# Two eight-expert stages on sorted rows, with their routing streamed behind the attention ahead of each

## The chip, the cores and the metric

The kernel runs on one core of a Trainium2 chip. The metric is the device time of one launch in microseconds (us). Engines are called as in the profile: PE (TensorE, matrix products; PEld is its weight load), DVE (VectorE), ACT (ScalarE), POOL (GpSimd), SP (SyncE, which issues most DMAs).

## The reference

Four layers run over x, 2048 tokens (8 x 256) of 128 channels. Each layer adds an attention and then a mixture of experts, both on a layer norm of x:

```python
x = x + _L1_xattn_ref(_layernorm(x), ctx, ctx, mask_bk, ...)   # 16 heads of 64, 64 keys
x = x + _L1_ffn_ref(_layernorm(x), ...)                        # 8 experts, F = 512, 2 picked
x = x + _L2_xattn_ref(_layernorm(x), ctx, ...)                 # 16 heads of 8, 64 keys
x = x + _L2_ffn_ref(_layernorm(x), ...)                        # 8 experts, F = 256, 2 picked
```

Layers 0 (narrow attention, self attention and four mixed experts) and 3 (two-way attention, 64 experts of which 6 are picked) are computed as before by both kernels. An eight-expert mixture is, for each token, the sum over its two picked experts i of

```python
h = silu(x @ w1[i]) * (x @ w3[i])
out = out + (h @ w2[i]) * wi[..., None]
```

where the two weights wi come from a softmax over the two highest gate logits.

## The kernel before

The tokens are 16 tiles of 128 rows, kept in SBUF as `x`. The program is a sequence of blocks. In a block each engine has its own program, written by hand, in the order in which it runs; engines wait for each other by semaphores, and a block ends when all its engines are done. Expert products use fp32r: each operand is split into a high part (ACT, a copy) and a low part (DVE, the difference), and three matmuls give the product.

The blocks around the change:

- `attend_wide` (L844), the attention of layer 1, runs over the tiles in steps, with stages of up to four later steps for one tile (`rotate`, L250, a loop). In one step PE does query products of tile t (L904), eight transposes of tile t-3 (L912, into a `ps_t` of 1024 columns), scores of tile t-1 (L922, L926), and the output product of tile t-4 (L936). DVE takes maxima and sums and ends with the add to `x` (L1018). POOL divides the softmax (`t_sm` times `t_den`, L892).
- `normalise` n5 then makes the layer norm of all rows (DVE L134, L167), turns it (PE L228), makes gate logits (PE L217), and loads the first expert weights.
- `experts_sorted` e1 (L2069): DVE picks two experts per token for all 16 tiles together (L2300 to L2316), PE counts them (L2194), DVE works out places and the table of blocks (L2320 to L2357). POOL then writes every row twice into a DRAM buffer, `sorted`, by 32 indirect DMAs (L2175), one per tile and pick. The buffer holds 39 blocks of 128 rows, each for one expert, and was filled with blank rows in the first attention (L2954). ACT and DVE (L2065, L2066) split the weights of eight experts meanwhile. When all rows have landed, SP loads batches of three blocks (`e_zb`, L2147). For each batch PE turns the rows (L2203) and they are split (DVE L2364). For each block PE multiplies up (L2215 to L2217), ACT does silu, DVE multiplies (L2374), PE turns the result (L2225), ACT and DVE split it, PE multiplies down (L2236 to L2240), DVE adds (L2387), and POOL writes the 128 rows back to the order of tokens by an indirect DMA (L2182). At the end SP reads them back (L2154) and DVE adds them to `x` (L2394).
- `open_small` n6 and `attend_small` t2 (L566) are the attention of layer 2, over eight sequences b of two tiles, with stages of up to three later steps. The last operation of a tile is DVE's add (L796).
- `normalise` n7 and `experts_gated` e2 (L1745) follow: every expert runs over all tokens in four groups of 512, with the gate multiplied in; the weights stream in and are split on the way.
- `normalise` n8 follows, and in it ACT splits the first piece of layer 3's expert weights (L2555), whose load SP issued in e2.

## Time and profile before

| | us |
|---|---|
| median of 3 runs | 1537.43 (1535.21 to 1538.8) |
| the profiled execution | 1535.73 |
| its span, first to last instruction | 1533.9 |
| attend_wide | 523.6 to 651.4 |
| n5, then e1 | 651.7 to 668.8, 669 to 870.8 |
| n6, then t2 | 872 to 892.8, 894 to 966.5 |
| n7, then e2 | 966.8 to 987.5, 987.8 to 1136.3 |

Busy time over the span is PE 1252.8 us (82%), DVE 954.1 (62%), ACT 717.2 (47%) and POOL 627.5 (41%); the mean granted clock of TensorE is 0.893 of full speed. These shares are averages over stages of different limits, so a stage is read by its own window. In a row of the timeline the bracket gives the idle time of that engine ahead of the instruction and what ended it.

### The profile page before, as it was taken

To read this page: it belongs to the slowest core of one execution; us is meant where nothing else is said; L and a number is where in the kernel's file an instruction comes from. 1 tells how busy PE (TensorE), PEld (TensorE's weight loads), DVE (VectorE), ACT (ScalarE), POOL (GpSimd) and SP (SyncE) were. 2 spreads that over 40 slices of the span, in tenths; PEclk is the share of its full clock that TensorE was granted. 3 is DMA by queue.
4 is the path that set the end of the run, shared out by engine and by line. 5 is a ranking of instruction groups with operands and counts; after the bars stand their busy time and mean duration, and the time that the engine had idled before them with its cause. 6 is when DMAs were issued, how large, how long until landed. Compare 5 with 4: busy or idle time off the path is not lost. (4 is left out here: it accounts for less than half of the span.)

```text
span 1533.9 us, 24119 instructions
## 1 busy us (share of the span) xinstructions
PE 1252.8 (82%) x7202; PEld 1023.8 (67%) x7202; DVE 954.1 (62%) x1956; ACT 717.2 (47%) x1258; POOL 627.5 (41%) x638
## 2 busy tenths in 40 slices
PE   5986489997997899930899489699968559999997
PEld 3873379996654599920788358588846447787875
DVE  5546688887324376561565555667767567677775
ACT  2444456675332445431455245355543435555553
POOL 3204444430000133227233332269947236666665
PEclk9997789998898899955899789699988679999998
DMA  7900010110000000032111260032213034343433
GB/s 199 223 1 0 13 45 26 41 36 6 0 1 0 21 2 0 0 130 88 40 46 41 65 163 1 21 100 91 79 57 128 1 90 127 114 128 119 124 116 103
DMA packets 77809, 99.14 MB, mean 65 GB/s; under 512 B 15242, under 2 KB 41741, under 8 KB 77722
## 3 DMA queue, kind: packets, MB, share of 16 engines
q1 hardware_dynamic: 74018, 92.95, 21.3%
q0 software_dynamic: 2272, 4.24, 0.8%
q10 hardware_dynamic: 1440, 0.98, 0.3%
q8 instruction: 39, 0.64, 0.2%
q14 instruction: 40, 0.33, 0.1%
HBM read 78.14 MB, written 14.16 MB: 60 GB/s over the span
## 5 line engine op out<-in xcount | busy, mean ns | idle before, releaser
L2742 POOL TENSOR_TENSOR e_h<-e_h,e_gate 128x512 f32<-128x512 f32 x128 | 187.8, 1484 | 135.4 <-DVE e_h L2794 87.3
L2799 DVE TENSOR_TENSOR e_h_low<-e_h,e_h_high 128x512 fp32r<-128x512 f32 x132 | 117.2, 888 | 77.5 <-ACT e_h_high L2729 77.3
L2729 ACT ACTIVATE e_h_high<-e_h 128x512 fp32r<-128x512 f32 x132 | 83.5, 633 | 102.8 <-POOL e_h L2742 94.7
L1320 PE MATMUL u_ps_o<-u_vaug,u_pT 128*128 128x72 f32 x768 | 97.1, 270 | 0.0
L2794 DVE TENSOR_TENSOR e_h<-e_s,e_ps_b 128x512 f32<-128x512 f32 x132 | 89.3, 677 | 10.3 <-ACT e_s L2714 5.5
L1320 PEld LDWEIGHTS u_ps_o<-u_vaug,u_pT 128*128 128x128 f32 x768 | 93.6, 192 | 0.0
L2714 ACT ACTIVATE e_s<-e_ps_a 128x512 f32<-128x512 f32 x132 | 77.5, 587 | 25.7 <-PE e_ps_a L1742 23.3
L1251 POOL TENSOR_TENSOR u_kbd<-u_keys,groupmask 96x512 fp32r<-96x512 f32 x60 | 62.8, 1067 | 62.5 <-DMA u_keys<-s_k 37.0
L1347 ACT ACTIVATE u_sm<-u_sm 128x512 f32<-128x512 f32 x96 | 60.6, 631 | 53.4 <-DVE u_sm L1379 52.8
L1377 DVE TENSOR_REDUCE u_mx<-u_ps_s 128x2 f32<-128x512 f32 (+1 forms) x96 | 66.2, 689 | 21.2 <-PE u_ps_s L1302 20.3
L228 PE MATMUL n_ps_t<-ident,n_zn 128*128 128x128 f32 x96 | 25.9, 433 | 61.6 <-DVE n_zn L167 53.8
L2182 POOL DMA_INDIRECT sorted_y<-e_y,e_zb x39 | 37.8, 970 | 91.2 <-DVE e_y L2387 88.7
L879 POOL MEMSET t_vbd<- 128x1024 f32 x1 | 1.0, 951 | 171.0 <-POOLq L816 171.0
L1379 DVE TENSOR_TENSOR u_sm<-u_ps_s,u_mx 128x512 f32<-128x512 f32 x96 | 66.4, 692 | 7.1
L1958 ACT ACTIVATE e_s<-e_ps_a 128x512 f32<-128x512 f32 x64 | 38.3, 599 | 58.3 <-PE e_ps_a L1742 58.3
L892 POOL TENSOR_TENSOR t_sm<-t_sm,t_den 128x1024 f32<-128x1024 f32 x16 | 30.4, 1901 | 82.3 <-DVE t_den L1004 82.3
L228 PEld LDWEIGHTS n_ps_t<-ident,n_zn 128*128 128x128 f32 x96 | 18.2, 226 | 67.3 <-DVE n_zn L167 59.2
L666 PE MATMUL t_ps_o<-a_vaug,t_pT 128*128 128x72 f32 x512 | 61.5, 273 | 0.0
L1343 ACT ACTIVATE u_pT<-u_ps_t 128x512 f32<-128x512 f32 x96 | 57.2, 595 | 8.3 <-PE u_ps_t L1308 6.4
L323 POOL TENSOR_TENSOR a_kbd<-a_k,groupmask 96x1024 fp32r<-96x1024 f32 x16 | 30.2, 1890 | 74.5 <-PE t_ps_t L653 60.3
L666 PEld LDWEIGHTS t_ps_o<-a_vaug,t_pT 128*128 128x128 f32 x512 | 59.9, 192 | 0.3
L1740 PE MATMUL e_ps_y<-e_h_high,ed_low 128*128 128x512 f32 x132 | 52.9, 400 | 8.5 <-DVE e_y L2803 5.5
(501 smaller groups left out, 3868.9 us busy)
## 6 DMA issues: line engine op xcount, KB each, us to landing
e_gate<-gates_by_expert SPq DMA_DIRECT2D x256, 128.0 KB, 2.9
e_gate<-gates_by_expert SPq DMA_DIRECT2D x32, 256.0 KB, 3.2
a_q<-q_part SPq DMA_DIRECT2D x24, 256.0 KB, 6.5
w_raw<-in_L1w SPq DMA_DIRECT2D x24, 256.0 KB, 4.1
u_qs<-s_q SPq DMA_DIRECT2D x16, 192.0 KB, 2.6
u_keys<-s_k SPq DMA_DIRECT2D x8, 384.0 KB, 3.5
w_w<-in_L2w SPq DMA_DIRECT2D x24, 128.0 KB, 2.6
sorted<-blank SPq DMA_DIRECT2D x1, 2535.0 KB, 16.5
```

Of the source, the lines that this page charges most:

```text
L666: last = nc.tensor.matmul(ps_o[:, a * NA:(a + 1) * NA], pT[b % 2][:, j, t * P:(t + 1) * P], vaug[b % 2][:, a, pair * NA:(pair + 1) * NA], ...
L1251: return eng.tensor_tensor(kbd[:, HG * g:HG * (g + 1), kb * P:(kb + 1) * P], keys[:, kb, g, :].unsqueeze(1).broadcast_to([ROWS, HG, P]), g ...
L1320: last = nc.tensor.matmul(ps_o[par][:, a * NA:(a + 1) * NA], pT[(r - 3) % 2][:, i, :], vaug[kb][:, a, own * NA:(own + 1) * NA], start=own ...
L1343: nc.scalar.activation(pT[r % 2][:, :, :].rearrange("p a b -> p (a b)"), ps_t[r % 2][:, :], ACT.Copy).then_inc(pT_ready, 1)
L1347: nc.scalar.activation(sm[r % 3][:, :], sm[r % 3][:, :], ACT.Exp, scale=scale).then_inc(p_ready, 1)
L1377: nc.vector.tensor_reduce(mx[r % 2][:, 0:heads], s3, X, ALU.max)
L1379: nc.vector.tensor_tensor(sm[r % 3][:, :].rearrange("p (h k) -> p h k", h=heads), s3, mx[r % 2][:, 0:heads].unsqueeze(2).broadcast_to([P, ...
L2714: nc.scalar.activation(s[c % 3][:, :], ps_a[c % 3][:, :], ACT.Silu).then_inc(s_ready, 1)
L2729: nc.scalar.activation(h_parts[k % 3][0][:, :], h[k % 3][:, :], ACT.Copy).then_inc(high_ready, 1)
L2742: nc.gpsimd.tensor_tensor(h[c % 3][:, :], h[c % 3][:, :], gate[pair % SLOTS][:, :], ALU.mult)\
L2794: nc.vector.tensor_tensor(h[c % 3][:, :], s[c % 3][:, :], ps_b[c % 3][:, :], ALU.mult)\
L2799: nc.vector.tensor_tensor(h_parts[k % 3][1][:, :], h[k % 3][:, :], h_parts[k % 3][0][:, :], ALU.subtract).then_inc(low_ready, 1)
```

## The change

A class `Router` splits the routing of an expert stage into steps for groups of four tiles. Each engine of the attention ahead calls it once per tile step t; tile t-4 is ready by then. The steps t = 0 to 19 of a group lie in the attention, the steps 20 to 27 at the start of `experts_sorted`:

```diff
+    def dve(self, dve, t):
+        if 4 <= t < TILES + 4:
+            dve.drain()
+            nc.vector.bn_stats(self.stats[:, t - 4, :], self.x[:, t - 4, :])
+        if t % 4 == 3 and 7 <= t < TILES + 4:
+            self.variance(dve, (t - 7) // 4)
+        if t % 4 == 0 and 8 <= t < TILES + 8:
+            self.normal_rows(dve, (t - 8) // 4)
+        if t % 4 == 2 and 10 <= t < TILES + 8:
+            self.pick(dve, (t - 10) // 4)
+        if t % 4 == 3 and 11 <= t < TILES + 8:
+            self.places(dve, (t - 11) // 4)
+        if t == TILES + 7:
+            self.block_table(dve)
...
+    def pool(self, pool, t):
+        if t % 4 == 0:
+            pool.wait_ge(self.index_ready, g + 1)
+            pool.wait_ge(self.copied, g + 1)
+        for k in range(PICKS):
+            self.nc.gpsimd.indirect_dma_start(
+                out=self.sorted_dram, out_offset=bass.IndirectOffsetOnAxis(ap=self.index[:, tile, k:k + 1], axis=0),
```

`Router.pe` turns a group's normal rows (t % 4 == 1), makes its logits (2) and its counts by five bf16 matmuls (3); `Router.act` makes the roots, copies the turned rows and the shares. POOL's step t sends tile t-12. So that a group can be placed before all tokens are counted, each expert has a fixed region of 2048 rows, and the table of blocks holds for each block the expert's weights and the row to read:

```diff
+REGION = B * S
+SORTED_ROWS = SORT_E * REGION + (SORT_E - 1) * P
...
-                src = sorted_dram[q * BATCH * P:(q + 1) * BATCH * P, :].rearrange("(b p) c -> p b c", p=P)
-                sp.dma_start(zb[q % NZ][:, :, :], src).then_inc(zb_loaded[q % NZ], 16)
+                for i in range(BATCH):
+                    j = q * BATCH + i
+                    row = sp.value_load(router.table[0:1, 1, j:j + 1], min_val=0, max_val=SORTED_ROWS - P)
+                    sp.dma_start(zb[q % NZ][:, i, :], sorted_dram[bass.ds(row, P), :]).then_inc(zb_loaded[q % NZ], 16)
```

`sorted` grows from 4992 to 17280 rows (8775 KB), there are two of them, and both are filled with blank rows at the end of the first attention's loads. Before e1's first product, PE makes eight dummy matmuls (`keep_busy`).

In `attend_wide` the loop is written out, `ps_t` is halved to free a bank of PSUM for the router, and a tile's transposes and copies go in two halves:

```diff
-        ps_t = m.ps("ps_t", 1024)
+        ps_t = m.ps("ps_t")
+            router.bank(m.ps("ps_n"))
...
-                    act.wait_ge(t_done, t - 2)
                     wait(act, o_done, t - 4)
-                    nc.scalar.activation(pT[1 - p][:, :, :].rearrange("p a b -> p (a b)"), ps_t[:, :], ACT.Copy)\
-                        .then_inc(pT_ready, 1)
+                    for half in range(2):
+                        act.wait_ge(t_done, 2 * (t - 3) + half + 1)
+                        nc.scalar.activation(pT[1 - p][:, 4 * half:4 * half + 4, :].rearrange("p a b -> p (a b)"),
+                                             ps_t[:, :], ACT.Copy).then_inc(pT_ready, 1)
```

The weights of `attend_wide` (2.1 MB) are loaded during n4, the layer norm ahead of it, and no longer in the first attention; a small block then waits for them. The first four experts' weights of e1 load during `attend_wide`. `normalise` n5 and n7 are gone.

In e2 `experts_gated` is replaced by `experts_sorted` with F = 256, 39 blocks. Its routing runs inside t2, where the ring of score banks falls from 3 to 2, three dummy matmuls stand in `turn_max` of the steps b >= 3, and at the end of the steps b = 1 to 8 ACT and DVE split one expert's weights each:

```diff
-    RING = 3
+    RING = 3 if router is None else 2
...
+                if router is not None and b >= 3:
+                    keep_busy(nc, ps_m, ones_b, 3)
                 pe.wait_ge(mx_ready, b + 1)
...
+                if weights is not None and 0 < b <= SORT_E:
+                    weights.make_low(dve, b - 1)
+                if router is not None and b > 0:
+                    router.dve(dve, TPB * (b - 1) + 1)
```

The load of layer 3's first weight piece is issued behind the reads of e2's results.

How the orders move at three places. PE in one step of `attend_wide`; `t_ps_t` takes the transposed softmax, `t_ps_s` the scores, `t_ps_o` the output. Before:

```order
L904 MATMUL t_ps_q<-zT,L1wq 128x128 x8
L912 MATMUL t_ps_t<-ident,t_sm 128x128 x8
L918 REGISTER_ALU
L922 ISA
L922 MATMUL t_ps_s<-neg,ident_b 128x512
L926 MATMUL t_ps_s<-t_kbd,t_qT 128x128 x4
L922 MATMUL t_ps_s<-neg,ident_b 128x512
L926 MATMUL t_ps_s<-t_kbd,t_qT 128x128 x4
L936 MATMUL t_ps_o<-t_vw,t_pT 128x128 x8
L39 REGISTER_ALU
L944 MATMUL t_ps_v<-L1wo,t_vbd 128x128 x4
```

Now, in a step in which the router turns a group (`t_ps_n`):

```order
L1217 MATMUL t_ps_q<-zT,a_L1wq 128x128 x8
L1233 MATMUL t_ps_t<-ident,t_sm 128x128 x4
L1238 MATMUL t_ps_s<-neg,ident_b 128x512
L1242 MATMUL t_ps_s<-t_kbd,t_qT 128x128 x4
L1233 MATMUL t_ps_t<-ident,t_sm 128x128 x4
L1238 MATMUL t_ps_s<-neg,ident_b 128x512
L1242 MATMUL t_ps_s<-t_kbd,t_qT 128x128 x4
L502 MATMUL t_ps_n<-ident,w_rows 128x128 x4
L1255 MATMUL t_ps_o<-t_vw,t_pT 128x128 x8
L1263 MATMUL t_ps_v<-a_L1wo,t_vbd 128x128 x4
L1217 MATMUL t_ps_q<-zT,a_L1wq 128x128 x8
```

The transposes stand in two halves, each ahead of a half of the scores, and the router's work stands between the scores and the output product.

DVE in one step b of t2; `t_mx` are maxima of the scores, `t_on` a tile's output, `x` takes the add. Before:

```order
L796 TENSOR_TENSOR x<-x,t_ps_w 128x128
L770 TENSOR_REDUCE t_mx<-t_ps_s 128x8 x2
L777 CAST a_mxs<-t_mx 128x2x16
L779 TENSOR_TENSOR a_mxs<-t_mx,a_mxs 128x2x16
L786 RECIPROCAL t_rden<-t_ps_o 128x16
L788 TENSOR_TENSOR t_on<-t_ps_o,t_rden 128x128
L796 TENSOR_TENSOR x<-x,t_ps_w 128x128
```

Now, in a step with the router's pick (`w_L` to `w_chosen`):

```order
L1095 TENSOR_TENSOR x<-x,t_ps_w 128x128
L1069 TENSOR_REDUCE t_mx<-t_ps_s 128x8 x2
L1085 RECIPROCAL t_rden<-t_ps_o 128x16
L1087 TENSOR_TENSOR t_on<-t_ps_o,t_rden 128x128
L351 BN_STATS w_stats<-x 128x6
L397 COPY w_L<-t_ps_n 128x32
L400 MAX w_best<-w_L 128x8 x4
L402 TENSOR_TENSOR w_apart<-w_best 128x4
L404 MAX_INDEX w_who<-w_best,w_L 128x8 x4
L406 CAST w_whof<-w_who 128x8
L409 TENSOR_TENSOR w_picked<-w_whof,number 128x4x8 x2
L413 TENSOR_TENSOR w_chosen<-w_picked 128x32
```

Statistics follow each add, and the pick stands ahead of the next step's add and maxima.

DVE at the start of e1. Before, the end of the routing, from the shares on (`e_index` are the places that the indirect DMAs use):

```order
L2347 TENSOR_REDUCE e_slot<-e_key 128x16
L2349 TENSOR_TENSOR e_share<-e_share,e_mx 128x16
L2351 CAST e_index<-e_slot 128x16
L2353 COPY w_rows<-e_share 128x16
L2354 COPY w_rows<-e_share 128x16
L2343 TENSOR_TENSOR e_key<-e_second,e_place 128x128
L2347 TENSOR_REDUCE e_slot<-e_key 128x16
L2351 CAST e_index<-e_slot 128x16
L2355 TENSOR_REDUCE e_expert<-e_passed 1x39
L2357 TENSOR_SCALAR e_table<-e_expert 1x39
L2065 TENSOR_TENSOR w_low<-w_raw,w_high 128x1024
L2066 TENSOR_TENSOR w_down<-w_raw,w_down 128x4x128
```

Now, from the block's first instruction:

```order
L381 TENSOR_TENSOR w_half<-w_root 128x4
L383 SCALAR_TENSOR_TENSOR w_half<-w_half,w_var 128x4
L386 SCALAR_TENSOR_TENSOR w_rstd<-w_half,w_root 128x4
L390 TENSOR_SCALAR w_rows<-x,w_mean,w_rstd 128x128 x4
L2388 TENSOR_TENSOR w_low<-w_raw,w_high 128x1024
L2389 TENSOR_TENSOR w_down<-w_raw,w_down 128x4x128
L397 COPY w_L<-e_ps_z 128x32
L400 MAX w_best<-w_L 128x8 x4
L402 TENSOR_TENSOR w_apart<-w_best 128x4
L404 MAX_INDEX w_who<-w_best,w_L 128x8 x4
L406 CAST w_whof<-w_who 128x8
L409 TENSOR_TENSOR w_picked<-w_whof,number 128x4x8 x2
```

Only the last group's normal rows and picks stand here, and one weight's low part ahead of the pick; its places (`w_index`), the table of blocks and the other seven weights' low parts follow in that order.

## Rows read from the trace of the kernel before

**Rows 1.** Windows: each stretch's length, busy time (instructions) of each engine, clock, DMA.

```profile
core 0: us, PE busy (x) PEld busy (x) DVE busy (x) ACT busy (x) POOL busy (x), PEclk, DMA share, GB/s
523.50:651.50 128.00, 122.50 (x1056) 120.07 (x1056) 84.25 (x96) 60.14 (x80) 39.77 (x35) 1.00 0.03 7
651.50:734.80 83.30, 12.38 (x68) 11.46 (x69) 33.33 (x99) 19.54 (x29) 40.66 (x38) 0.52 0.32 108
734.80:856.00 121.20, 116.77 (x738) 102.02 (x738) 73.92 (x129) 66.81 (x130) 36.86 (x38) 0.96 0.12 35
856.00:872.00 16.00, 0.00 (x1) 0.03 (x1) 5.54 (x8) 0.04 (x1) 1.01 (x2) 0.50 0.48 132
894.00:966.50 72.50, 65.35 (x480) 55.69 (x480) 37.92 (x96) 33.14 (x72) 17.92 (x22) 0.97 0.22 51
966.50:1137.50 171.00, 152.73 (x656) 123.62 (x656) 124.76 (x204) 83.94 (x149) 121.37 (x113) 0.90 0.25 78
```

**Rows 2.** Timeline, from e1's first indirect DMA to its first product (start, length, instruction).

```profile
681.20 1.20 POOL L2175 DMA_INDIRECT sorted<-w_rows,e_index  x1 [9.54 <-DVE e_index L2351]
...
682.70 6.60 POOL L2175 DMA_INDIRECT sorted<-w_rows,e_index  x1 [0.30 <-issue]
...
727.75 0.97 POOL L2175 DMA_INDIRECT sorted<-w_rows,e_index  x1 [0.30 <-issue]
...
730.10 1.44 SPq L2147 DMA_DIRECT2D e_zb<-sorted  x3
...
734.81 0.79 PE L2215 MATMUL e_ps_a<-w_high,e_z_low 128*128 x1 [1.25 <-DVE e_z_low L2364]
```

**Rows 3.** Timeline, PE: transposes in attend_wide, gate products in n5, counts in e1.

```profile
591.63 1.04 PE L912 MATMUL t_ps_t<-ident,t_sm 128*128 128x128 f32 x8
...
665.05 3.42 PE L217 MATMUL n_ps_g<-gate,zT 128*128 128x8 f32 x16
...
674.60 1.03 PE L2194 MATMUL e_ps_z<-e_chosen,ones_b 128*128 128x120 bf16 x15
```

**Rows 4.** Lines, DVE: normal rows of 651 to 735, maxima of 1219 to 1246.

```profile
L167 DVE TENSOR_SCALAR w_rows<-x,n_mean,n_rstd 128x128 f32<-128x128 f32 x16 | 4.3, 342 | 0.2
...
L2760 DVE MAX8 e_top<-e_grp 128x8 f32<-128x12 f32 x16 | 1.3, 157 | 0.1
```

**Rows 5.** Timeline, DVE: the low part of a weight in e1.

```profile
681.43 1.21 DVE L2065 TENSOR_TENSOR w_low<-w_raw,w_high 128x1024 fp32r<-128x1024 f32 x1
...
687.77 0.67 DVE L2066 TENSOR_TENSOR w_down<-w_raw,w_down 128x512 fp32r<-128x512 f32 x1
```

**Rows 6.** Lines, e1's blocks, 735 to 856: count, busy us, mean ns, idle ahead and releaser.

```profile
L2182 POOL DMA_INDIRECT sorted_y<-e_y,e_zb x38 | 36.9, 970 | 89.9 <-DVE e_y L2387 87.5 <-issue 2.4
...
L2374 DVE TENSOR_TENSOR e_h<-e_s,e_ps_b 128x512 f32<-128x512 f32 x39 | 26.8, 688 | 32.2 <-PE e_ps_b L2217 31.0 <-PE e_ps_h L2225 1.1
...
L2215 PE MATMUL e_ps_b<-w_high,e_z_low 128*128 x39 | 16.1, 412 | 0.0
...
L2364 DVE TENSOR_TENSOR e_z_low<-e_ps_z,e_z_high 128x384 fp32r<-128x384 f32 x12 | 6.7, 557 | 3.5 <-ACT e_z_high L2269 2.3
```

**Rows 7.** Timeline, e1's end: the last block's sum, the reads of the results, the last adds.

```profile
855.62 0.35 DVE L2387 SCALAR_TENSOR_TENSOR e_y<-e_ps_y,e_zb,e_part 128x128 f32<-128x128 f32 x1 [1.83 <-ACT e_part L2291]
...
858.94 5.97 SPq L2154 DMA_DIRECT2D w_rows<-sorted_y  x8
...
867.81 2.99 DVE L2394 TENSOR_TENSOR x<-x,w_rows 128x512 f32<-128x512 f32 x4 [0.42 <-DMA w_rows<-sorted_y]
```

**Rows 8.** Timeline, ACT at the start of n8.

```profile
1137.49 1.08 ACT L2555 ACTIVATE eg_high<-eg_raw 128x1056 fp32r<-128x1056 f32 x1 [10.51 <-PEq L70]
```

**Rows 9.** DMA issues: the filling of `sorted` before (count, KB, us to landing).

```profile
sorted<-blank SPq DMA_DIRECT2D x1, 2535.0 KB, 16.5
```

**Rows 10.** Timeline, SP: the issue of the filling, and the first load of the self attention.

```profile
56.48 0.47 SPq L2954 DMA_DIRECT2D sorted<-blank  x1
...
188.75 0.63 SPq L1235 DMA_DIRECT2D u_qs<-s_q  x1
```

More of the change, by code:

```diff
@@ L613, in _ @@
                     nc.gpsimd.tensor_tensor(x[:, t, :], x[:, t, :], w["bo"][:, :], ALU.add).then_inc(bias_added, 1)
+            if router is not None:
+                router.first_pool(pool)
+                for t in range(TILES + LAGS):
+                    router.pool(pool, t)
         @block.tensor
@@ L718, in _ @@
                     project(TPB * (b - 2))
+                if router is not None and b > 0:
+                    router.pe(pe, TPB * (b - 1) + 1)
         @block.scalar
@@ L752, in _ @@
                     max_rows(b - 1)
+                if router is not None and b > 0:
+                    router.act(act, TPB * (b - 1))
                 if 0 <= b - 3 < B:
@@ L763, in _ @@
                     exponentials(b - 1, 3)
+                if weights is not None and 0 < b <= SORT_E:
+                    if b == 1:
+                        for g in range(GROUPS):
+                            act.wait_ge(st.q_stored[g], 32)
+                    weights.make_high(act, b - 1)
+                if router is not None and b > 0:
+                    router.act(act, TPB * (b - 1) + 1)
         @block.vector
@@ L804, in _ @@
                     divide(TPB * (b - 2))
+                if router is not None and b > 0:
+                    router.dve(dve, TPB * (b - 1))
                 if 0 <= b - 3 < B:
@@ L908, in step @@
                     pe.wait_ge(p_ready, t - 2)
-                    wait(pe, pT_ready, t - 3)
-                    tile = sm[(r - 3) % 4]
-                    for j in range(8):
-                        last = nc.tensor.transpose(ps_t[:, j * P:(j + 1) * P],
-                                                   tile[:, 2 * j:2 * j + 2, :].rearrange("p a b -> p (a b)"), ident)
-                    last.then_inc(t_done, 1)
                 if live(t, 1):
@@ L2139, in _ @@
         def _(sp):
-            weights.later_loads(sp)
+            if not weights.split_ahead:
+                weights.later_loads(sp)
+            sp.wait_ge(router.table_ready, 1)
             sp.wait_ge(scattered, 16 * PICKS * TILES)
@@ L2362, in z_part @@
+            router.dve(dve, TILES + 6)
+            router.dve(dve, TILES + 7)
+            if not weights.split_ahead:
+                for e in range(1, E):
+                    weights.make_low(dve, e)
             def z_part(q):
@@ L3005, in build @@
             experts_mixed(nc, "e0_", x, x2, self_w, zT, logits[4], rank)
+        early.close()
         clear_spent(nc)
[L3008 to L3014 removed]
@@ L3050, in build @@
         finish()
+        late.close()
+        narrow.close()
 def lay_out(i):
```

579 lines of the change are left out of this document (375 added, 204 removed).

## The prediction

> **What bounds the kernel now.** The chain that ended last runs through the final stage alone, so it prices nothing here; I read the program by windows, one per stage [rows 1], and then the timeline across each gap. The reader should see two kinds of stage. In the wide attention PE is busy 122.5 of 128 us at full clock: it is bound by PE, and DVE (84.25) and POOL (39.77) have room. Between that attention and e1's first product lie 83.3 us in which PE is busy 12.4 at a granted clock of 0.52: there the chain is layer norm, routing, POOL's indirect DMAs and the first batch. The narrow attention t2 lies between: PE 65.35 and DVE 37.92 of 72.5. From its end to n8 it takes 171 us, of which PE works 152.7: the dense experts are bound by PE, and what shortens them is fewer products.
>
> The profiled execution took 1535.73 us, 1.7 under the median of 1537.43 and inside its three runs; the sum is made against it. A measurement of this kernel tells about 0.2% (3 us) from no change.
>
> **The wide attention grows: +17.5 us (8 to 32).** The router gives PE, for a group of four tiles, four transposes at 1.04/8, four gate products at 3.42/16 and five counts at 1.03/15 [rows 3]: 0.52 + 0.86 + 0.34 = 1.7 us, for three groups 5. On DVE a group costs four normal rows at 0.342 and eight maxima and their places at 0.157 [rows 4], four statistics (some 0.3 each) and about 25 small operations, which I price like the maxima: 1.4 + 1.3 + 1.2 + 4.0 = 8 us. With 3.25 groups inside the steps that is 26, so DVE comes to 110 of some 140: not the bound on average, but it runs in order, and a pick of about 2.6 us stands ahead of the next tile's maxima. I give 3 us for that, and 3 for the halved `ps_t`, where PE waits for ACT's copy between the halves, about 0.2 for each of 16 tiles. The end is not covered: between and after the last adds stand a pick (2.6), a variance (0.9), places (1.9) and the waits between them, 6.5 in all. 5 + 3 + 3 + 6.5 = 17.5. The lower end is PE's 5 with half the tail; the upper has DVE's stalls in every step, one more us for most tiles. POOL's two DMAs per tile from step 12 on cost 2 x (0.97 + 0.30) us [rows 2]; with its 39.77/16 = 2.5 us per tile [rows 1] it fits into an 8 us step.
>
> **From that attention to e1's first product: 83.3 becomes 35, -48.3 us (30 to 43).** n5 and the routing of all tiles go. What is left is the chain of the last group: root 0.8, normal rows with three small operations 1.9, turning and the copy some 2, gate products 0.9 and a wake, pick 2.6, counts 0.8, places 1.9, together about 12 us until POOL has the last places. POOL has 16 DMAs left; eight run beside this chain, the other eight from 12 on: 8 x 1.27 = 10.2, with a wake 22.7. From the end of the last one (728.72) to SP's load took 1.4, and from SP's load to the first product 4.7 [rows 2]. SP now reads a row number ahead of each of three DMAs; no row shows that, so I bound it by nothing and by a SP issue of 0.5 each [rows 10], and take 0.6 each with the wait on the value, for 1.8. That gives 30.6. Then the low parts: DVE splits eight weights at 1.21 + 0.67 [rows 5] beside the scatter. One DMA beside them took 6.60 us, not 0.97, and all 32 took 47.5 us, from 681.20 to 728.72, where 32 x 1.27 is 40.6: 6.9 more [rows 2]. I take 4 of these: 35. The window also shows POOL's DMAs, not the splitting, setting its end, so the low parts (15 us) are hidden unless the scatter gets shorter than they are.
>
> At that place the Trainium skill (SBUF — State Buffer, "Who interferes with whom") has a rule against this change: a DVE instruction with two SBUF inputs and a GpSimd instruction that reads SBUF share a port pair that one of them locks for its whole length, and a DMA of GpSimd's queue may starve for it. The trace shows it at most in part: one of 32 was 6.60, and the 38 scatters inside the blocks, beside a busy DVE, had a mean of 0.970 [rows 6]. By the rule in full, all eight weights would hold POOL up, 15 us in place of 4, and the sum would be 1490.6.
>
> **Clock: -2.3 us (-4.8 to 0).** In the blocks' 121.2 us the clock was 0.96 on average [rows 1], so some 4.8 us were lost after the idle wait; eight dummy matmuls in the wait may give back about half.
>
> **t2 grows: +25 us (10 to 45).** PE gets 5 for the router and 15 dummy matmuls; each is at most the 0.41 of a 512-column row [rows 6], and I take 3.5 in all. 65.35 + 8.5 is 74; with its idle 7 us kept, 81, so +8.5. The tail is the same 6.5. DVE gets the 26 of the router and eight half-sized low parts, 8 x 0.94 = 7.5: 37.9 + 33.5 = 71.4, as long as the whole stage was. DVE and PE both full, each in order and with two banks for the scores in place of three: I give 10 for steps in which PE waits for maxima behind a pick or behind a low part that itself waits for ACT's high one. 8.5 + 6.5 + 10 = 25. The lower end has none of these stalls and a short tail; the upper has them in each of eight steps, 3 us more.
>
> **From t2's end to n8: 171 becomes 119, -52 us (-68 to -37).** The first product comes after 31, as in e1, without the low parts. A block of F = 512 took 121.2/39 = 3.11, with PE busy 2.99 [rows 1]. At F = 256 all but the turning of the input is halved; one transpose a block, 1.04/8 = 0.13 [rows 3], so PE needs 1.56. DVE needs 73.92/39 = 1.90 now; its operations on h halve (two of about 0.69), the sum of 0.35 and a third of the 0.557 of the input stay [rows 6, 7]: about 1.2. So PE would bound at 1.56 and the old pitch bounds from above; I take 1.75, nearer the PE row, since every third block has the turning and splitting of a batch in the way. 39 x 1.75 = 68, 4 to fill. Then the end: from 855.97 to 872, 16 us, for loads, adds and a block's end [rows 1, 7], the same size. 31 + 72 + 16 = 119. The ends are blocks at 1.56 and a 26 us start, and 2.1 with a start of 36.
>
> **Two loads moved.** The first weights of layer 3 are issued after the reads of e2's results, so ACT's split, which waited for nothing but the block at n8's start [rows 8], may wait for three large loads: +3 (0 to 6). The 2.1 MB of `attend_wide`'s weights load inside the 13 us of n4; the filling moved 2535 KB in 16.5 [rows 9], so 13.7, and a block more to wait for them: +1 (0 to 4). The larger filling, 2 x 8775 KB at that rate, is 114 us from 56: it ends at 170, ahead of the first load that could meet it, 188.75 [rows 9, 10]: nothing; if it were a third slower, 15 more.
>
> **Sum:** 17.5 - 48.3 - 2.3 + 25 - 52 + 3 + 1 = -56.1; 1535.7 - 56.1 = **1479.6 us**, own range 1462 to 1497.
>
> **Rivals.** *DVE bounds both attentions.* The picks and low parts stall every step: +32 and +45 in place of 17.5 and 25, so 1514. For it: DVE's 71.4 of 72.5 in t2, in order. Against: in the wide attention 30 us stay free.
> *The covers hold.* The attentions grow by 8 and 10, the blocks run at 1.56: 9.5 + 15 + 7 less, 1448. For it: DVE was idle for half of t2; against: the uncovered tails.
> *The filling is late.* 1495, as above.
> *The routing isn't hidden.* One late wait makes the groups slip to the expert stages; then 16 more DMAs per stage lie in the open, 20 us each: 1520. Against: the steps are four or more behind the tiles that they need.
> *Slower: the indirect DMAs are slow beside a busy DVE.* If each took the 6.60 [rows 2], POOL would need 2.5 + 2 x 6.9 = 16.3 us in an 8.2 us step of the wide attention, and its division would hold PE up: 8 x 8.1 = 65. In t2 the 16 DMAs stand behind POOL's other work, in the last 36 us, and need 110: 74 more. 1479.6 + 139 = 1619. In the wide attention it decides from (8.2 - 2.5)/2 - 0.3 = 2.6 us per DMA; the kernel is slower than before from about 4.0. Against: 0.97 is the rule in both groups of rows.
>
> **How the numbers follow.** Forecast 0.53, DVE 0.19, the covers hold 0.17, filling late 0.04, routing not hidden 0.03, slow DMAs 0.04. The range 1444 to 1516 takes in the first three and leaves out the two worst and the ends of the unknown costs. All but the last give faster by over 0.2%: faster 0.95, within 0.2% 0.01, slower 0.04.
>
> **What would show it.** In the changed profile: `attend_wide` about 145 us long; e1's first product about 35 us behind it; t2 near 97; e2's first product 31 behind, and its blocks at a pitch of 1.75. Indirect DMAs of 0.97 in the attentions speak against the slow rival, DVE idle ahead of its maxima against the DVE rival. The forecast is wrong if an attention grows beyond 35 us, if e2's pitch is beyond 2.1, or if a load of the self attention starts later.

## The result, and the profile after

The changed kernel took 1520.05 us in the median of four runs (1506.52 to 1526.98), the kernel before 1536.32 beside it (1532.44 to 1538.8): a ratio of 0.9891, 95% interval 0.9855 to 0.9927. It is faster by 16 us where 56 were forecast, and its time lies above the range given (1444 to 1516). The profiled execution took 1518.92 us, its span 1517.1. By stages of the two profiled executions, an attention counted to the end of its block:

| us | before | after | forecast | measured |
|---|---|---|---|---|
| up to `attend_wide` | 523.5 | 522.1 | +1 | -1.4 |
| `attend_wide` | 127.8 | 154.2 | +17.5 | +26.4 |
| its end to e1's first product | 83.4 | 38.5 | -48.3 | -44.9 |
| that to n6 | 137.1 | 131.5 | -2.3 | -5.7 |
| n6 | 22.1 | 22.3 | 0 | +0.2 |
| t2 | 72.5 | 119.2 | +25 | +46.7 |
| its end to n8 | 171.0 | 130.6 | -52 | -40.4 |
| n8 to the end | 396.4 | 398.6 | +3 | +2.2 |

The windows of the kernel after, answering to [rows 1] (t2 in four stretches, then e2's start, blocks and end):

```profile
core 0: us, PE busy (x) PEld busy (x) DVE busy (x) ACT busy (x) POOL busy (x), PEclk, DMA share, GB/s
522.10:676.30 154.20, 132.04 (x1107) 127.51 (x1107) 106.40 (x249) 68.47 (x112) 56.17 (x53) 0.97 0.11 34
676.30:714.80 38.50, 7.30 (x29) 4.06 (x29) 23.18 (x67) 15.76 (x24) 22.32 (x16) 0.55 0.37 119
868.70:890.00 21.30, 16.65 (x85) 10.58 (x84) 9.90 (x17) 7.44 (x14) 7.05 (x10) 0.90 0.96 222
890.00:913.00 23.00, 22.57 (x103) 21.01 (x102) 11.97 (x29) 9.03 (x19) 6.69 (x6) 0.51 0.14 43
913.00:950.00 37.00, 30.37 (x234) 26.70 (x233) 29.69 (x114) 18.57 (x45) 10.12 (x12) 1.00 0.11 33
950.00:987.90 37.90, 28.77 (x128) 25.63 (x128) 17.67 (x107) 11.15 (x27) 11.96 (x12) 0.50 0.07 24
987.90:1019.20 31.30, 7.79 (x29) 4.27 (x29) 9.31 (x51) 3.71 (x8) 15.67 (x16) 0.50 0.15 45
1019.20:1102.70 83.50, 72.03 (x387) 55.85 (x387) 47.81 (x129) 44.66 (x129) 36.94 (x38) 0.96 0.19 54
1102.70:1118.50 15.80, 0.00 (x0) 0.00 (x0) 5.55 (x9) 0.00 (x0) 0.99 (x2) 0.53 0.75 232
```

The reader should look at the clock first. In t2 it was 0.97 before; now it is 0.51 from 890 to 913 and 0.50 from 950 on, that is, at the lower of its two levels (1.2 of 2.4 GHz) for 61 of 119 us. In the first of these PE is busy for 22.57 of 23.00 us: nothing but its own speed holds the stage there. What stands ahead of it, in the timeline of ACT and of PE:

```profile
886.80 0.63 ACT L2382 ACTIVATE w_high<-eg_raw 128x512 fp32r<-128x512 f32 x1 [6.57 <-DMA eg_raw<-in_L2w]
...
888.83 1.22 PE L937 MATMUL t_ps_t<-a_q,a_kbd 128*128 128x256 f32 x4 [3.41 <-ACT a_q L1012]
```

The change lets ACT split an expert's weight from step b = 1 on. That weight had not landed (its load stood on SP behind those of `a_q`, and the DMA share up to 890 is 0.96), ACT waited 6.57 us for it, and `a_q`, the copy that the scores need, stood behind on ACT's queue. PE paused, and its clock fell. Ahead of the second fall, the timelines of PE and ACT:

```profile
944.24 0.30 PE L958 MATMUL t_ps_w<-ident,t_on 128*128 128x128 f32 x1 [2.09 <-DVE x L1095]
...
947.68 0.48 PE L937 MATMUL t_ps_t<-a_q,a_kbd 128*128 128x256 f32 x2
```

```profile
950.61 0.60 ACT L1021 ACTIVATE t_pT<-t_ps_t 128x512 f32<-128x512 f32 x1 [4.25 <-remote]
```

The first is a variance and the places of a group (941.46 to 943.87 on DVE), ahead of the add that PE waits for. The second is ACT's exponential of the scores, which is late for no cause that the profile names: the product that it reads (947.68) ended at 948.16, 2.45 us ahead of it. POOL's first indirect DMA in t2 is at 944.86.

The gap behind the wide attention, answering to [rows 2], in the timelines of POOL, DVE, SP and PE:

```profile
689.80 0.97 POOL L535 DMA_INDIRECT sorted<-w_rows,w_index  x1 [2.45 <-DVE w_index L435]
...
693.64 7.02 POOL L535 DMA_INDIRECT sorted<-w_rows,w_index  x1 [0.30 <-issue]
...
699.13 0.67 DVE L2389 TENSOR_TENSOR w_down<-w_raw,w_down 128x512 fp32r<-128x512 f32 x1
...
705.43 0.97 POOL L535 DMA_INDIRECT sorted<-w_rows,w_index  x1 [0.31 <-issue]
...
708.80 7.46 SPq L2460 DMA_DIRECT2D e_zb<-sorted  x7
...
714.78 0.79 PE L2502 MATMUL e_ps_a<-w_high,e_z_low 128*128 x1 [1.25 <-DVE e_z_low L2609]
```

The last eight start 13.5 after the block's end (676.3; 12 and a wake forecast) and take 16.6 us instead of 8 x 1.27 = 10.2, for one of 7.02 among them and two of 1.3; from their end to the first product it is 8.4 (1.4 + 4.7 + 1.8 = 7.9 forecast).

The indirect DMAs inside the wide attention, and those inside t2, by lines:

```profile
L535 POOL DMA_INDIRECT sorted<-w_rows,w_index x16 | 16.0, 999 | 4.0 <-issue 4.0
```

```profile
L535 POOL DMA_INDIRECT sorted<-w_rows,w_index x16 | 16.0, 1000 | 35.5 <-DVE w_index L435 31.3 <-issue 4.3
```

They were nearly as short as in [rows 6] (0.970). e2's blocks by lines, 1019 to 1103:

```profile
L2502 PE MATMUL e_ps_a<-w_high,e_z_low 128*128 x39 | 20.0, 512 | 7.7 <-issue 4.1 <-DVE e_h L2617 2.2 <-DVE e_z_low L2609 1.3
L2504 PE MATMUL e_ps_a<-w_high,e_z_high 128*128 x39 | 16.1, 414 | 0.0
```

The first product of a block takes 512 ns where its twin takes 414, and PE stood idle in front of it, 4.1 us of it for nothing that the profile shows.

### The profile page after: what moved, and what is told of

Same layout as the page of the kernel before. It is cut to its first block and busy times, and to the rows that moved or that the text cites. A ratio compares the mean times of both kernels' runs of the same rounds, so it can differ in the third digit from the quotient of the medians.

```text
span 1517.1 us, 24504 instructions
## 1 busy us (share of the span) xinstructions
PE 1215.3 (80%) x7038; PEld 987.4 (65%) x7038; DVE 937.4 (62%) x2232; ACT 698.4 (46%) x1306; POOL 576.4 (38%) x594
## 5 line engine op out<-in xcount | busy, mean ns | idle before, releaser
L2972 ACT ACTIVATE e_h_high<-e_h 128x512 fp32r<-128x512 f32 x132 | 83.5, 633 | 102.9 <-POOL e_h L2985 94.8
L2478 POOL DMA_INDIRECT sorted_y<-zT,e_zb x78 | 75.8, 972 | 144.3 <-DVE zT L2630 137.0
L535 POOL DMA_INDIRECT sorted<-w_rows,w_index x64 | 70.0, 1093 | 71.3 <-DVE w_index L435 35.4
L2957 ACT ACTIVATE e_s<-e_ps_a 128x512 f32<-128x512 f32 x132 | 77.6, 588 | 27.5 <-PE e_ps_a L2071 25.3
L950 PE MATMUL t_ps_o<-a_vaug,t_pT 128*128 128x72 f32 x512 | 73.7, 306 | 0.1
L228 PE MATMUL n_ps_t<-ident,n_zn 128*128 128x128 f32 x80 | 21.3, 433 | 65.3 <-DVE n_zn L167 57.4
L950 PEld LDWEIGHTS t_ps_o<-a_vaug,t_pT 128*128 128x128 f32 x512 | 72.0, 224 | 0.5 <-issue 0.3
L228 PEld LDWEIGHTS n_ps_t<-ident,n_zn 128*128 128x128 f32 x80 | 14.9, 224 | 69.8 <-DVE n_zn L167 61.7
```

The source lines that it names most:

```text
L535: self.nc.gpsimd.indirect_dma_start(out=self.sorted_dram, out_offset=bass.IndirectOffsetOnAxis(ap=self.index[:, tile, k:k + 1], axis=0), i ...
L950: last = nc.tensor.matmul(ps_o[:, a * NA:(a + 1) * NA], pT[b % 2][:, j, t * P:(t + 1) * P], vaug[b % 2][:, a, pair * NA:(pair + 1) * NA], ...
L2478: nc.gpsimd.indirect_dma_start(out=y_dram, out_offset=bass.IndirectOffsetOnAxis(ap=at, axis=0), in_=y[j % NY][:, :], in_offset=None, bound ...
L2957: nc.scalar.activation(s[c % 3][:, :], ps_a[c % 3][:, :], ACT.Silu).then_inc(s_ready, 1)
L2972: nc.scalar.activation(h_parts[k % 3][0][:, :], h[k % 3][:, :], ACT.Copy).then_inc(high_ready, 1)
```

## Experiments

Each ratio is to the kernel before, in runs beside it. The first five change one thing in the changed kernel; from the seventh on, each edit stands on the run that is named. In the diffs, `...` marks lines left out. Stage lengths are those of the profiled execution; in this section t2 is counted to its last add (116.6 in the changed kernel, 72.5 before). One profile of a stage doesn't fix its length to the microsecond: t2 as in the changed kernel took 116.6, 120.2 and 113.5 (the changed kernel, runs 3 and 5), and t2 as in run 2 took 96.5 and 99.4 (runs 2 and 6).

**1. The splitting later.**

```diff
-                if weights is not None and 0 < b <= SORT_E:
-                    weights.make_high(act, b - 1)
+                if weights is not None and 3 <= b < SORT_E + 3:
+                    weights.make_high(act, b - 3)
```

(the same for `make_low` on DVE).

> Weight splitting in the narrow attention t2 moved two steps later (steps b = 3 to 10 in place of 1 to 8), nothing else. Theory C (the clock): t2 took 119 us in place of 72.5 because TensorE fell to half clock twice, from 890 to 913 after a pause in which ACT waited 6.6 us for the first weight at the end of step 1, and from 950 to the end. With the weight long there, the first pause and the first slow stretch go: t2 shorter by 13 to 18 us, the granted clock 1.00 until late in t2, the kernel 1502 to 1508. Rival D (DVE is the bound of t2 at any clock, by its 71 us of work in order): the same work on DVE in other steps, t2 shorter by the 6.6 us of the wait at most, or not at all: 1513 to 1520.

Measured: 1504.53 us, ratio 0.9791 (0.9767 to 0.9814). t2 took 103.4, and the first fall of the clock is gone. Windows of t2:

```profile
870.60:935.00 64.40, 56.42 (x397) 46.09 (x398) 45.51 (x143) 33.06 (x73) 20.10 (x25) 0.98 0.40 100
935.00:974.10 39.10, 33.44 (x151) 30.09 (x149) 19.84 (x103) 13.24 (x32) 15.02 (x16) 0.50 0.12 38
```

The wait for the weight that had not landed, and the clock behind it, cost 13 us; the second fall stays.

**2. No splitting in t2.** The weights are split at e2's start, as in e1, and five of the eight are loaded there too.

```diff
-                             loads=weights.all_loads, router=router, weights=weights)
+                             loads=weights.first_loads, router=router)
+            weights.split_ahead = False
```

> No weight splitting inside t2: the eight weights of e2 are split at the start of e2, beside the indirect DMAs, as e1 does it. Theory C: the first slow stretch goes as in the run with late splitting; the second, which begins behind the router's variance and places on DVE, stays or comes a step later: t2 shorter by 13 to 20 us; e2's start grows by up to 8 us, since low parts stand beside the indirect DMAs (one of 7 us in e1). Kernel 1505 to 1512. Rival D: DVE loses 8 us of work, t2 shorter by about 8, e2's start longer by as much: 1518 to 1522.

Measured: 1504.52 us, 0.9788 (0.9765 to 0.9812). t2 took 96.5; e2's first product came 37.1 after the last add, 34.2 in the changed kernel. So the splitting in t2, with the loads that go with it, cost 20 us there and saved 3.

**3. The register read ahead.** PE reads a block's weight offset one block early.

```diff
-                    offs[j] = nc.tensor.value_load(router.table[0:1, 0, j:j + 1], min_val=0, max_val=(E - 1) * weights.span)
...
+                    if j + 1 < BLOCKS:
+                        offs[j + 1] = read_off(j + 1)
```

> In both sorted stages PE reads the weight offset of a block one block ahead, behind the previous block's first products, in place of right ahead of its own. Theory V: e2's pitch was 2.05 us, not the 1.75 that was forecast, because PE stops about 0.3 us a block for that read (the first product of a block had a mean of 512 ns where the same matmul otherwise has 412, and an idle time of 0.2 to 0.4 ahead of it): pitch 1.75 to 1.85, e2 shorter by 8 to 12 us, e1 by 0 to 2. Rival L: the loop from the product down over ACT's and DVE's operations, in order, back to the next product down sets the pitch: it stays at 2.0 to 2.05 and the time within 2 us of 1520.

Measured: 1513.53 us, 0.9843 (0.9816 to 0.987). From e2's first to its last product up it took 69.8 us, 78.6 in the changed kernel: 0.23 for each of 38 pitches, now 1.84. The time fell by less (6.5 us), for t2 took 120.2 in this profile. By lines, 1025 to 1100 (the first two blocks begin ahead of 1025):

```profile
L2502 PE MATMUL e_ps_a<-w_high,e_z_low 128*128 x37 | 14.7, 397 | 0.0
```

No idle time is left ahead of the first product. In e1 the same edit changed nothing: from its first to its last product up it took 108.8 us, 108.9 in the changed kernel.

**4. The first half of the change alone.** t2, n7 and the dense experts as before.

```diff
-                             loads=weights.all_loads, router=router, weights=weights)
-            experts_sorted(nc, "e2_", x, weights, idn, ones_b[:, :], router, rows, drams[1], signals[1],
...
+            normalise(nc, "n7_", x, idn, root_ln, zT, gate_w=gate2, logits=logits[8], then=ACT.Exp, parts=z,
...
+            experts_gated(nc, "e2_", x, z, logits[8], rank, weights, idn, gates_dram, zT,
```

> Only the first half of the change: t2, the layer norm n7 and the dense experts of e2 as before; the wide attention with e1 streamed as in the change. From the stages of the changed kernel (t2 +46.7, t2's end to n8 -40.4) the second half costs 6 us: the kernel 1511 to 1516, with t2 at 72 to 73 us. If the two halves hang together (the clock, the loads, the filling of the second buffer), it comes out elsewhere: under 1508 or over 1520.

Measured: 1512.32 us, 0.985 (0.9823 to 0.9877), t2 73.6 and 171.3 from there to n8. By the medians the second half of the change cost 8 us where the forecast had it save 24; the intervals of the two ratios overlap a little.

**5. The router out of the wide attention.** All its steps run at e1's start; the written-out loop and the halved `ps_t` stay.

```diff
+            if router.whole:
+                for t in range(TILES + LAGS):
+                    router.pe(pe, t)
```

(the same for DVE, ACT and POOL).

> The wide attention without the router: its loop, its halved ps_t and its loads as in the change, and all routing steps of e1 run in the same order at e1's start. What the router costs and saves there alone: theory R (the router's work on DVE and PE makes the attention's 23 to 25 us): the attention takes 128 to 133 us in place of 151, and the stretch from its end to e1's first product grows from 41 to 80 to 90 (four chains of about 12 us for the groups, POOL's 32 indirect DMAs behind them): kernel 1532 to 1545. Rival P (the halved ps_t alone costs most of it, PE waiting for ACT's copy between the halves): attention 140 or more, kernel over 1545.

Measured: 1540.94 us, 1.0042 (1.0025 to 1.0059). To the last add the attention took 132.4 us (127.8 before, 151.3 in the changed kernel), and the gap behind it 80.6 (41.4 there). Alone the loop costs 4.6; the router costs 19 in the attention and saves 39 behind it. In this profile the self attention ended some 8 us later than elsewhere, for which I have no cause.

**6. Edits 2 and 3 together**, their diffs as above.

> Weights of e2 split at e2's start and weight offsets read one block ahead, together. If the two costs are separate (one a wait of ACT and DVE work in t2, the other a stall of PE per block), the gains add: 1520 less 15.5 less 6.5 is 1498, 1495 to 1501. If e2's blocks are then bound by something else that the shorter start exposes, 1501 to 1505.

Measured: 1495.48 us, 0.9737 (0.9707 to 0.9768); t2 99.4, e2's products 70.1. The two add up.

**7. Four more dummy matmuls** (on 6) in each of the steps b = 4 to 8.

```diff
+                if router is not None and 4 <= b <= B:
+                    keep_busy(nc, ps_m, ones_b, 4)
```

> On top of the two cures, four more dummy matmuls in each step b = 4 to 8 of t2, ahead of the turning of a tile's output, where PE waits. Theory C: the second slow stretch of TensorE (from about 935 to the end of t2) begins after such pauses; with them filled the clock stays at 1.00 until the last steps: t2 8 to 12 us shorter than in the run with two cures, kernel 1486 to 1491. Rival D: the pauses are DVE's lateness and the dummies add up to 4 us: t2 0 to 4 longer, kernel 1498 to 1503.

Measured: 1496.59 us, 0.9746 (0.9699 to 0.9792); t2 99.8, its clock 0.88 (0.81 in 6). No gain.

**8. The places a step later** (on 6), so that variance and places don't stand in one step.

```diff
+        if t % 4 == 0 and 12 <= t <= TILES:
+            self.places(dve, (t - 12) // 4)
-        if t % 4 == 3 and 11 <= t < TILES + 8:
-            self.places(dve, (t - 11) // 4)
...
```

> On top of the two cures, the router's places move one step later (beside the next normal rows), except a stage's last ones, so that no step of DVE holds a variance, a pick and places together; nothing is added. Theory D: DVE's heaviest steps make PE late in both attentions: wide 2 to 4 us shorter, t2 4 to 8 shorter, and the clock may stay up for it: kernel 1488 to 1494. Theory C without D: the pauses that lower the clock stay as often, the time within 3 us of the run with two cures.

Measured: 1494.96 us, 0.974 (0.9712 to 0.9767); not told from 6 by its time. The wide attention took 150.5 (152.1 in 6). t2 took 96.7 (99.4 in 6, but 96.5 in 2).

**9. All 32 indirect DMAs of e2 at its start** (on 8): POOL sends none in t2.

```diff
-                for t in range(TILES + LAGS):
-                    router.pool(pool, t)
...
```

> As the run with spread places, but all 32 indirect DMAs of e2's routing at e2's start, none in t2. Does POOL's work in t2 bring the second slow stretch, which began within 3 us of its first indirect DMA in four kernels? Theory M (it does): clock at 1.00 until the last steps, t2 82 to 88 us; e2's start grows by 16 x 1.27 = 20. Theory C (pauses of PE behind DVE's late steps do): the slow stretch stays, t2 within 3 us of 96.7, the kernel 1512 to 1518.

Measured: 1502.49 us, 0.9796 (0.9771 to 0.9822). t2 took 86.4, 10.3 less than in 8, at a clock of 0.94 (0.85); e2's first product came 56.9 behind, 17.6 later. Up to POOL's first indirect DMA (932.35 in 8) the two profiles run alike, 8 some 2.6 us later. Then, in 8, in the timelines of PE, DVE and ACT:

```profile
935.71 1.96 PE L953 MATMUL t_ps_o<-a_vaug,t_pT 128*128 128x72 f32 x16
```

```profile
940.94 0.26 DVE L1088 RECIPROCAL t_rden<-t_ps_o 128x16 f32<-128x16 f32 x1 [4.77 <-remote]
```

```profile
943.84 0.28 ACT L1039 ACTIVATE t_onT<-t_ps_w 128x128 f32<-128x128 f32 x1 [6.46 <-remote]
```

And in 9, the same two steps of PE and DVE:

```profile
933.14 1.96 PE L951 MATMUL t_ps_o<-a_vaug,t_pT 128*128 128x72 f32 x16
```

```profile
935.14 0.26 DVE L1086 RECIPROCAL t_rden<-t_ps_o 128x16 f32<-128x16 f32 x1 [1.54 <-PE t_ps_o L951]
```

With the DMAs DVE starts 3.3 us behind the end of PE's products, without them at once; the "remote" is where the profile has no releaser. PE then waited 5.26 us for that ACT copy.

**10. Without the change's own dummies** (on 8).

```diff
-                if router is not None and b >= 3:
-                    keep_busy(nc, ps_m, ones_b, 3)
```

> As the run with spread places, without the three dummy matmuls of the change in t2's steps b = 3 to 8. Theory C: less work of PE in its pauses, the clock falls earlier, t2 2 to 10 us longer. Theory D: the dummies are in the way, 0.64 us a step: t2 0 to 4 us shorter.

Measured: 1501.08 us, 0.9769 (0.9729 to 0.9808), runs from 1493.8 to 1506.92; t2 102.0 at a clock of 0.72. The interval overlaps with that of 8: unclear.

**11. Many more dummies** (on 8): six at three places of every step from b = 6.

```diff
+                if router is not None and b >= 6:
+                    keep_busy(nc, ps_m, ones_b, 6)
...
```

> As the run with spread places, with six dummy matmuls (1.3 us at full clock) at three places in each of t2's steps b = 6 to 10, ahead of the projections and of a turning. Theory C: if the pauses that lower the clock lie at these places, the clock stays at 1.00 to the end of t2, which takes 86 to 92 us: kernel 1484 to 1490. If they are only in the way (DVE sets the pace of these steps, or the clock falls all the same): t2 97 to 108, kernel 1495 to 1506.

Measured: 1498.13 us, 0.977 (0.9745 to 0.9794). The clock in t2 rose to 0.95, and t2 took 101.6. The late starts stayed, at full clock: PE's products of 938.62 end at 940.57, and DVE takes them up 4.1 us later:

```profile
944.69 0.26 DVE L1094 RECIPROCAL t_rden<-t_ps_o 128x16 f32<-128x16 f32 x1 [6.84 <-remote]
```

So the late starts don't come from the clock, and filling PE's time costs what the clock gives.

**12. t2 without the router** (on 8), two banks for the scores as in the change; all routing at e2's start.

```diff
-    RING = 3 if router is None else 2
+    RING = 2 if spare_bank or router is not None else 3
...
-                             loads=weights.first_loads, router=router)
+                             loads=weights.first_loads, spare_bank=True)
...
+            router.whole = True
```

> t2 without router, dummies and splitting, with two score banks as in the change; all routing steps of e2 run at e2's start, with the two cures and spread places else. Tells the router's price in t2 and what streaming saves behind it. Theory R (router work makes t2's growth): t2 73 to 77 us at full clock; from its end to e2's first product 75 to 85, in place of 39. Rival P (two banks in place of three cost most): t2 over 85. By R the kernel comes to 1512 to 1520: streaming into t2 saves some 20 us, and e2 on sorted rows without it is no faster than the dense experts.

Measured: 1507.09 us, 0.982 (0.9793 to 0.9846). Windows of t2, and from there to e2's first product:

```profile
868.50:941.10 72.60, 65.11 (x480) 55.53 (x478) 38.41 (x96) 33.25 (x72) 17.91 (x22) 0.98 0.28 65
941.10:1015.40 74.30, 16.89 (x79) 12.16 (x79) 39.01 (x220) 26.20 (x47) 34.98 (x34) 0.54 0.20 60
```

To the last add t2 took 72.9, 72.5 before with three banks: the third bank was worth nothing. The router, with the change's dummies, costs 24 us in t2 (96.7 in 8) and saves 35 behind it.

**13. The DMAs of t2 held back** (on 8): POOL waits for tile t-4's add before the two of step t.

```diff
+                    if t >= 12:
+                        pool.wait_ge(x_done, t - 3)
```

> As the run with spread places, but in t2 POOL waits for the add of a tile before its next two indirect DMAs, so that they go two per step and not eight in a row. Theory M (a burst of POOL's DMAs holds up what waits for PE, and the clock falls behind that): t2 84 to 91 us in place of 96.7, with its first slow stretch later or gone; since a part of the sixteen then ends later, e2's start may grow by 0 to 4; kernel 1485 to 1492. Rival (any indirect DMA there, or a pause that only fell on that moment): t2 94 to 100, kernel 1493 to 1500.

Measured: 1492.48 us, 0.9717 (0.9698 to 0.9736), the lowest time here, though its interval overlaps with those of 8 and 14; t2 93.4, less than in 8 by about as much as two profiles of the same t2 differ. The wait spread the DMAs only in part: six of the first eight still began within 6.5 us.

**14. The same in the wide attention too** (on 13), the two lines of 13 in its POOL program.

```diff
+                    if t >= 12:
+                        pool.wait_ge(x_done, t - 3)
```

> The same pacing in the wide attention too, where the last six indirect DMAs stand in a row and the add of tile 14 came 2.2 us behind its product. Theory M: wide 147 to 149 us in place of 150.5, else as the run paced in t2: 1482 to 1491. Rival: wide unchanged, or longer by up to 3 where POOL's waits make its division late.

Measured: 1493.45 us, 0.9722 (0.9703 to 0.9742): the attention 148.7, 1.7 less than in 13, and the gap behind it 45.1, 2.4 longer. Nothing gained.

**15. POOL busy, without the DMAs** (on 9): 48 clearings of a small tile in the places of the sixteen DMAs.

```diff
...
+                    for k in range(3 * PICKS):
+                        pool.drain()
+                        nc.gpsimd.memset(idle[:, :], 0.0)
```

> Edit: the kernel in which all 32 indirect DMAs of e2 are issued at e2's start (late_dma), with POOL clearing a small SBUF tile 48 times in the places of t2 at which it would have issued its sixteen DMAs, behind the same waits. Theory E (an engine POOL that is occupied, or that touches SBUF then, delays the others): t2 grows from late_dma's 86.4 toward 96.7, the length with the DMAs in place. Theory D (it is the DMAs themselves): t2 stays at 86 to 88, and no DVE instruction of the last steps starts more than 3 us behind the product that it waits for. Time by E some 1512, by D 1502 to 1504.

Measured: 1506.61 us, 0.9832 (0.9815 to 0.9849). The last add came 87.4 after t2's start, 86.4 in 9. POOL was busy for 20.1 us with them, and DVE was on time:

```profile
936.09 0.26 DVE L1093 RECIPROCAL t_rden<-t_ps_o 128x16 f32<-128x16 f32 x1 [1.54 <-PE t_ps_o L958]
```

**16. DMAs of SP in the same places** (on 9): it writes sixteen tiles of 128 rows to a spare buffer that nothing reads.

```diff
+                        sp.dma_start(spare_dram[n * P:(n + 1) * P, :], router.rows[k][:, t - 12, 0:D]).then_inc(spared, 16)
...
```

> Edit: the kernel in which all 32 indirect DMAs of e2 are issued at e2's start (late_dma), with SP writing sixteen tiles of 128 rows of the same normal rows to a spare DRAM buffer by direct DMAs, behind the same two waits at which POOL would have sent its sixteen. Theory T (the traffic of 128 rows in rows of 512 bytes is what delays DVE and ACT behind PE's products): the adds of t2 end near 96 behind its start, as with the indirect DMAs, and DVE or ACT instructions of the last steps start over 3 us behind their product. Theory G (it is tied to the indirect DMAs of POOL): the last add stays 86 to 88 behind the start, as without any DMA and as with the memsets (87.4), and no such instruction is late. Time by T some 1512, by G 1502 to 1505.

Measured: 1502.55 us, 0.9818 (0.977 to 0.9865); t2's last add 87.0 after its start, and again no late start:

```profile
933.77 0.26 DVE L1098 RECIPROCAL t_rden<-t_ps_o 128x16 f32<-128x16 f32 x1 [1.54 <-PE t_ps_o L963]
```

Neither an occupied POOL nor that much traffic does it: the 10 us come with POOL's indirect DMAs themselves. What in them holds up others was not found.

## Why the prediction was wrong

**t2, +25 forecast, +46.7 measured: the step that failed.** To the last add, t2 grew by 44, and the runs split it: 20 for the splitting (run 2), 10.3 for the indirect DMAs (runs 9, 15 and 16, on run 8), and 13.5 for the rest of the router with the dummies (run 9's 86.4 against run 12's 72.9), each to within some 3 us. The 8.5 of PE's work and the 6.5 of the tail, 15 together, were about that rest and the 2.6 behind the last add; the two were not measured apart. The "10 for steps in which PE waits" stood for the splitting, and it was twice that: I had the low part wait for ACT's high one, and didn't ask what ACT's high one waits for. It was a load behind nine others on SP; what is queued behind a waiting ACT (`a_q`) set PE's pause, and PE's products at half clock came on top. Pause and half clock together are 13 of the 20 (run 1). The working held the clock of 0.97 through a stage to which it added pauses. The DMAs I had priced by POOL's time alone, as work that fits in; they held up DVE and ACT instead, which no row of before showed at that place.

**e2, -52 forecast, -40.4 measured.** The start was right (31.3 after the block's end, 31 forecast) and so was the end (15.8, 16 forecast). The pitch failed: "39 x 1.75 = 68, 4 to fill" was 83.5 in all, a pitch of 2.04, and 0.23 of the 0.29 is the register that PE reads for each block ahead of its first product. The kernel before has the same read, and in its e1, with blocks of 3.11 us, it shows no price; by lines, 735 to 856, of before:

```profile
L2215 PE MATMUL e_ps_a<-w_high,e_z_low 128*128 x39 | 16.5, 424 | 1.3 <-DVE e_z_low L2364 1.3
```

There the read is covered, as it is in the changed kernel's own e1 (run 3); in halved blocks it isn't. My step halved the work of a block and didn't ask what its length had hidden. With the read out of the way the pitch is 1.84 (run 3).

**The wide attention, +17.5 forecast, +26.4 measured.** Inside the range given, in its upper half. Of the 26.4, the written-out loop and the halved `ps_t` take 4.6 (3 forecast), the router 18.9 up to the last add and 2.9 behind it (run 5; 14.5 forecast, tail included). The tail is what was small. From the add of tile 11 to that of tile 15 it was 18.1 us without the router (run 5) and 30.0 with it, and 2.9 lie behind: 14.8 where the term was 6.5. Up to tile 11 the router cost 7.0, where 8 were forecast. Timeline of DVE in run 5:

```profile
644.62 0.28 DVE L1346 TENSOR_TENSOR x<-x,t_ps_o 128x128 f32<-128x128 f32 x1
...
662.75 0.29 DVE L1346 TENSOR_TENSOR x<-x,t_ps_o 128x128 f32<-128x128 f32 x1 [2.21 <-PE t_ps_o L1256]
```

The timelines of DVE and PE in the changed kernel:

```profile
643.13 0.28 DVE L1345 TENSOR_TENSOR x<-x,t_ps_o 128x128 f32<-128x128 f32 x1
...
666.21 0.29 DVE L1345 TENSOR_TENSOR x<-x,t_ps_o 128x128 f32<-128x128 f32 x1 [7.89 <-remote]
...
673.11 0.29 DVE L1345 TENSOR_TENSOR x<-x,t_ps_o 128x128 f32<-128x128 f32 x1 [4.01 <-PE t_ps_o L1255]
```

```profile
669.15 0.21 PE L516 MATMUL t_ps_n<-w_chosen,ones_b 128*128 128x32 bf16 x1 [5.14 <-DVE w_chosen L413]
```

Tile 14's add came 2.2 us behind its product (which ended at 664.0), again beside indirect DMAs, the pick stood behind it, and PE waited 5.14 for the pick with the last tile's product queued behind the counts. Holding the DMAs back there made the attention 1.7 shorter (run 14); a run without them was not made, so their share of the tail stays open.

**The gap, -48.3 forecast, -44.9 measured.** Its size held, and its mechanism but for one reading. The term "4 of these" for indirect DMAs beside low parts was 6.4 (16.6 less 10.2), 6.05 of it in the one DMA of 7.02. I took such a DMA for an exception; the last section shows that it lasts as long as the low parts beside it follow one another without a pause.

**The small terms.** -2.3 for the clock in e1 was -5.7: from the first to the last product up the blocks take 108.9 in place of 114.0, at a clock of 0.99 in place of 0.96. No run took the dummies ahead of them out, so the clock's share is not shown. ACT's split of layer 3's first weights does wait for its load now, but it starts only 1.0 us after n8's start (1118.5), where it had started with it [rows 8]; 3 were forecast, and the stretch behind n8 grew by 2.2:

```profile
1119.53 1.08 ACT L2798 ACTIVATE eg_high<-eg_raw 128x1056 fp32r<-128x1056 f32 x1 [17.22 <-DMA ed_raw<-in_L3ed]
```

`attend_wide` begins 1.4 us earlier than before: neither its weights nor the filling was late.

**The rivals.** "DVE bounds both attentions" named +32, +45 and 1514. Its sizes were close in t2, its mechanism not: at half clock PE is busy for 22.57 of 23.00 us while DVE has 11.97. "The routing isn't hidden" named 1520, the time that came out, by luck: no group slipped, for each attention holds 16 indirect DMAs as planned. "The indirect DMAs are slow" is out in the attentions (0.999 and 1.000 us each). Its price was looked for on POOL; what the DMAs cost in t2 is paid by DVE and ACT. Of the prediction's own signs of being wrong one came: t2 grew beyond 35 us. The errors add up: 21.7 for t2, 11.6 for e2, 8.9 and 3.4 for the wide attention and its gap, less 6.4 for the small terms, is the 39 that the span (-16.8) misses of -56.1.

## What to carry to other kernels

Work that is streamed into a stage brings its waits along: before an operation is put on an engine's queue, ask when its input lands and which instruction of the stage stands behind it, for a pause of PE can be paid a second time by its clock. When blocks are made shorter, ask of each small step (here a register read) what in the longer block had covered it; reading one block ahead bought it back. No splitting in t2 and the read ahead, with places a step later and the DMAs held back, give 1492.48 us, 0.9717 (0.9698 to 0.9736) of the kernel before, against 0.9891 for the change; of the four the first two carry most of the gain (0.9737 in run 6).
